# A Mamba-plus-cross-attention kernel on one Trainium2 core: TensorE's order inside a pair of units is alternated

## The reference, cut to what matters

```
for l in range(4):                      # Mamba layers
    x = rmsnorm(h); xi, z = split(x @ in_proj)
    xi = silu(causal_conv4(xi)); dt, B, C = split(xi @ x_proj); dt = softplus(dt @ dt_proj + b)
    for t in time:                      # 512 channels x 16 states
        s = exp(dt*A) * s + dt*B*xi     # the scan
        y = sum over the 16 states of s*C
    h = h + ((y + xi*D) * silu(z)) @ out_proj
h = rmsnorm(h)[:, 64:, :]
x = h + attention(layernorm(h), layernorm(ctx)) @ Wproj; x = x + mlp(layernorm(x))
```

## Time and profile before

| | |
|---|---|
| median of 3 runs | 9717.55 us (9715.33 to 9719.66) |
| the profiled execution, its own time | 9715.03 us |
| its span from first to last instruction | 9712.9 us |
| PE / DVE / ACT / POOL busy | 8902.0 / 7467.3 / 5988.0 / 6846.0 us |
| mean granted TensorE clock | 0.962 of full speed |

### The profile page before, as it was taken

The page is one execution under the profiler, slowest core; times in us unless marked ns, Lnnn a source line. Parts: engine busy times, 40 slices in busy tenths (PEclk is TensorE's granted clock), DMA queues, the critical chain, the costliest instruction groups (busy, mean ns, idle before and its releaser), DMA issues.

```text
span 9712.9 us, 193419 instructions
## 1 busy us (share of the span) xinstructions
PE 8902.0 (92%) x67488; PEld 6194.1 (64%) x67488; DVE 7467.3 (77%) x7810; ACT 5988.0 (62%) x9252; POOL 6846.0 (70%) x5860
## 2 busy tenths in 40 slices
PE   8999799999997899999997799999988799999988
PEld 5666466677664567677664566776654576766654
DVE  5778588888873588888873588888873688888872
ACT  6666576667753576676743566677642566776642
POOL 5888588888861488888861488888861588888850
PEclk9999899999999899999999899999999899999999
DMA  1111111111100111111100111111100111111100
GB/s 56 46 46 41 45 51 39 42 39 51 48 33 5 57 42 39 42 43 55 39 33 6 57 42 39 42 52 46 39 32 8 55 42 39 51 49 41 39 33 9
DMA packets 132829, 390.42 MB, mean 40 GB/s; under 512 B 49520, under 2 KB 77620, under 8 KB 94984
## 3 DMA queue, kind: packets, MB, share of 16 engines
q1 hardware_dynamic: 131848, 377.75, 10.9%
HBM read 364.46 MB, written 13.24 MB: 39 GB/s over the span
## 4 chain that ended last, share of the span: by engine, by line
POOL 51%; issue 36%; PE 3%; POOLq 1%; DVE 1%; ACT 0%; DVEq 0%; ACTq 0%
POOL arena L1139 43%; POOL arena L1146 4%; POOL arena L1158 2%; PE ps L540 1%; POOL arena L1176 1%; POOLq L1136 1%; PE ps L621 1%; DVE arena L1080 0%; DVE arena L1071 0%; ACT arena L824 0%; PE ps L517 0%; PE ps L587 0%; PE ps L437 0%; PE ps L616 0%; PE ps L454 0%
## 5 line engine op out<-in xcount | busy, mean ns | idle before, releaser
L1139 POOL TENSOR_TENSOR arena<-arena 128x512 f32<-128x512 f32 x4608 | 5765.3, 1276 | 1143.4 <-DVE arena L912 1103.9
L912 DVE TENSOR_TENSOR_SCAN arena<-arena,ps 128x512 f32<-128x512 f32 x4608 | 5610.4, 1259 | 785.6 <-PE ps L437 600.8
L673 ACT ACTIVATE arena<-arena,rate 128x512 f32<-128x512 f32 (+1 forms) x4608 | 3100.3, 713 | 801.8 <-DVE arena L912 789.8
L437 PE MATMUL ps<-arena 64*128 64x128 f32 x36864 | 2710.8, 287 | 313.8 <-DVE arena L912 306.4
L437 PEld LDWEIGHTS ps<-arena 64*128 64x128 f32 x36864 | 2266.9, 189 | 745.9 <-DVE arena L912 445.9
L454 PEld LDWEIGHTS ps<-csts,arena 128*128 128x128 f32 x18432 | 2128.5, 143 | 849.1 <-issue 629.5
L454 PE MATMUL ps<-csts,arena 128*128 128x128 f32 x18432 | 2466.4, 277 | 28.1 <-POOL arena L1139 27.4
L1158 POOL TENSOR_TENSOR arena<-arena 128x512 f32<-128x512 f32 x288 | 365.6, 1269 | 777.4 <-DVE arena L957 777.4
L1146 POOL TENSOR_TENSOR arena<-csts,arena 128x512 f32<-128x512 f32 x576 | 603.3, 1049 | 76.4 <-ACT arena L764 76.4
L517 PE MATMUL ps<-arena 128*128 128x512 f32 x1152 | 639.2, 649 | 7.6 <-DVE arena L962 4.4
L484 PE MATMUL ps<-arena 128*128 128x512 f32 x1152 | 636.0, 643 | 2.7 <-DVE arena L940 2.7
(11 more groups left out here) (102 smaller groups left out, 7510.2 us busy)
## 6 DMA issues: line engine op xcount, KB each, us to landing
arena<-c_rows SPq DMA_DIRECT2D x288, 1024.0 KB, 4.7
arena<-ip_x SPq DMA_DIRECT2D x20, 512.0 KB, 3.6
arena<-ip_z SPq DMA_DIRECT2D x20, 512.0 KB, 3.7
arena<-op_w SPq DMA_DIRECT2D x20, 512.0 KB, 3.8
hT<-xT SPq DMA_DIRECT2D x16, 512.0 KB, 5.1
arena<-w SPq DMA_DIRECT2D x8, 1024.0 KB
out<-arena SPq DMA_DIRECT2D x64, 128.0 KB, 1.7
arena<-xp_w SPq DMA_DIRECT2D x20, 160.0 KB, 2.4
```

Of the source, the lines that this page charges most:

```text
L437: i = nc.tensor.matmul(o, dtxT[rows, c, b, :], diagB[rows, pair, b, :].rearrange("p (i s) -> p i s", s=2), start=True, stop=True)
L673: nc.scalar.activation(o, i, ACT.Exp, scale=rate[:, ph.layer(n), g:g + 1]).then_inc(decay.sem, 1)
L912: nc.vector.tensor_tensor_scan(hs[:, place(n, v) + g % 2, :], dA[:, g % RING, :], both[:, g % 2::2], init[:, n % 2, g:g + 1] if ph.main() ...
L1139: nc.gpsimd.tensor_tensor(hs[:, a, :], hs[:, a, :], Crep[:, g % DS, :], ALU.mult).then_inc(prod.sem, 1)
```

## The change

TensorE's list alternates. In even units it stays: input of v+1, jobs of v, sum of v-2. In odd units it is turned round: sum of v-2, jobs of v, input of v+1. Nothing is added or removed, and no other engine's list is touched.

```
             def body(ph, n):
                 for v in range(UNITS):
-                    to, w = ahead(ph, n, v + 1)
-                    if to is not None:
-                        make_input(ph, to, w)
+                    ahead_of, behind = ahead(ph, n, v + 1), ahead(ph, n, v - 2)
+                    if ahead_of[0] is not None and v % 2 == 0:
+                        make_input(ph, *ahead_of)
+                    if behind[0] is not None and (scans(ph, n) or n == ph.steps) and v % 2:
+                        sum_pair(ph, *behind)
                     for m, name in events(ph.pe_at, ph, n, v):
                         job(ph, m, name)
-                    to, w = ahead(ph, n, v - 2)
-                    if to is not None and (scans(ph, n) or n == ph.steps):
-                        sum_pair(ph, to, w)
+                    if behind[0] is not None and (scans(ph, n) or n == ph.steps) and v % 2 == 0:
+                        sum_pair(ph, *behind)
+                    if ahead_of[0] is not None and v % 2:
+                        make_input(ph, *ahead_of)
```

## The result

The changed kernel takes 9861.24 us (median of 4 runs, 9860.55 to 9865.58), the kernel before 9718.6: ratio 1.0148, interval 1.013 to 1.0165. It is 1.5% slower. The forecast was 9783 us, 0.7% slower: right in direction and inside the range, but with less than half of the loss (65 of 143 us).

What follows compares the result with a forecast made beforehand. TensorE was taken to bound most of a main step, VectorE about a quarter. The profiled 9715 + 19 (main) + 31 (pre) + 15 (clock) = 9780, with 2.5 more for the median 9783 us; range 9685 to 9890.

Steps and rivals of the forecast that it cites:

- the order of events at units 14 to 17: Main step: input 16 comes 5.65 us after input 14, input 17 at 7.9 after 1.3 us of new idle time.
- trip: TensorE going into 64-row input matmuls and out again: about 0.4 us each, bounds 0.30 to 0.45; 16 instead of 32 a step.
- the undisturbed main step: Main step: 110.0 less 6.4 saved plus 6.7 new waits gives 110.3 us, +19 us over 64 steps.
- The waits of TensorE: Main step, ahead of inputs 3, 5, 7, 9, 17, 23, 25, 29, 31: 11.6 us instead of 4.9.
- The saving: TensorE's joints, every main and pre step: 16 x 0.4 = 6.4 us saved, bounds 4.8 to 7.2.
- the pre phase: 8 pre steps: each grows from 118.7 to 122.6 us by the sum, +31 us in all, bounds +16 and +60.
- The lump behind `out`: Pre step: input 6 moves from 695.27 to 702.9 behind the `out` jobs, making the scans of unit 7 2.1 us late.
- rival D: Main step: late GpSimd products stall sums ahead of an input, up to 0.5 us a step; 9815 us, chance 0.1.
- the clock: Main steps: new idle time brings some more half-speed stretches, 15 at 1 us each, +15 us.
- rival C: A half-speed stretch in each main step, where TensorE has no slack: 46 to 146 us more, 9860 us; chance 0.17.
- its sign, a mean clock under 0.95: Whole kernel: a mean TensorE clock below 0.95 would show the forecast wrong and point to rival C.
- the ends of the blocks: Last main steps and attention: no separate term; all 64 main steps at 0.3 us each, attention parts unchanged.

Runs made afterwards that it cites:

- e4: The changed kernel plus 14 unread identity transposes ahead of the input of unit 31, in all main steps but each block's last; 9789.56 us (1.0073).
- e10: The old order everywhere, plus 8, 10 and 8 unread identity transposes in units 4, 5 and 7 of each main step; 9706.94 us (0.9989).
- e11: The changed kernel with each block's last main step and the units that drain it put back in the old order; 9828.29 us (1.0114).
- e3: The kernel before with only units 7, 9, 11, 15 and 17 of each main step turned round, pre in the old order; 9614.9 us (0.9892).
- e6: The kernel before with the even units turned round instead of the odd ones, in both phases; 10115.5 us (1.0413).
- e7: The kernel before with units 4 to 10, 14, 16, 18 turned in main and 7, 10, 17, 18 in pre; 9730.54 us (1.0014).

## Why the prediction was right and wrong

**Right: the order of events at units 14 to 17.** The prediction put input 16 at 5.65 us behind input 14, and input 17 at 7.9 with 1.3 us idle. The timeline of PE in the changed kernel:

```profile
1406.50 1.91 PE L454 MATMUL ps<-csts,arena 128*128 128x128 f32 x16
1408.25 0.60 PE L510 MATMUL ps<-csts,arena 128*128 128x128 f32 x4
...
1409.64 2.06 PE L437 MATMUL ps<-arena 64*128 64x128 f32 x32
...
1415.29 1.16 PE L437 MATMUL ps<-arena 64*128 64x128 f32 x16
1417.58 1.16 PE L437 MATMUL ps<-arena 64*128 64x128 f32 x16 [1.13 <-DVE arena L915]
```

Input 16 comes at 5.65, input 17 at 7.94 with 1.13 us idle; two sums take 1.75 us, that is 2 x 0.88. In the old order input 17 comes 6.04 us behind input 15, with two jobs of the same kind and two sums between them (1601.72 to 1607.76 in the step of the earlier trace rows), so here one trip less is worth 0.39 us.

**Right by luck: the undisturbed main step.** The forecast was 110.0 - 6.4 + 6.7 = 110.3; measured are 110.6 (e4, at a clock of 1.00) against 110.0 (e10). But both terms were too large, and their errors nearly cancel. The waits of TensorE in that step of e4:

```profile
L437 PE MATMUL ps<-arena 64*128 64x128 f32 x514 | 35.9, 282 | 6.8 <-DVE arena L920 6.8
...
L490 PE MATMUL ps<-arena 128*80 128x512 f32 x8 | 3.9, 608 | 1.6 <-DVE arena L965 1.6
```

With 0.2 us ahead of `ms` and the 1.7 us that the filler covers they are 10.3 us, 5.5 more than the 4.8 of before and not 6.7 more. They stand where the forecast put them, ahead of the inputs 3, 5, 7, 17, 23 and 31, but for input 9: there the `xp` job waits in its place, for a bank, which the forecast did not have. The saving is what was mis-sized more: TensorE is busy 102.0 us, 100.3 without the filler, against 105.2, so 4.9 us are saved and not 6.4, that is 0.31 us a trip and not 0.4, at the lower end of the forecast's bounds. Why a trip is worth less on average than at units 14 to 17 no run shows.

Over the first 15 steps of the blocks the turned order costs 40 us (6628.6 in e4, 6588.4 in e10), where 64 steps were to give 19. Some 31 of it are the 0.6 us of 13 steps a block; about 5 lie in the first step of each block (109.7 against 108.5) and about 5 in the stretches that e4 still has.

**Right in its sum, with a wait that it did not have: the pre phase,** 29.8 us against 31, within the 8 us by which executions with this list differ, and 122.5 a step against 122.6. The lump behind `out` is there: in the timeline of DVE in a pre step of the changed kernel the scans of unit 6 start 6.53 us after the last of unit 5; the row gives no releaser, but their input starts at 722.70, behind the `out` jobs, and they follow it by 1.26.

```profile
714.00 3.43 DVE L915 TENSOR_TENSOR_SCAN arena<-arena,ps 128x512 f32<-128x512 f32 x3
723.96 1.22 DVE L915 TENSOR_TENSOR_SCAN arena<-arena,ps 128x512 f32<-128x512 f32 x1 [6.53 <-issue]
```

The input of unit 6 comes later than forecast, 10.9 us behind that of unit 5 and not 9.7, because the sum of unit 3, which now stands ahead of the jobs, waits for its product:

```profile
710.77 2.33 PE L437 MATMUL ps<-arena 64*128 64x128 f32 x32
...
715.24 0.66 PE L454 MATMUL ps<-csts,arena 128*128 128x128 f32 x4 [0.57 <-POOL arena L1142]
```

This is the mechanism of rival D, which the prediction looked for in the main steps. Up to the first main step the sums wait 45.6 us for GpSimd, against 11.5 before; in the first 15 steps of the first block it is 0.6 us.

**Wrong: the clock.** This is the term that was mis-sized: "I expect some more such stretches: 15 at 1 us each, **+15 us**". The prediction had found the idle time (2.2 us at unit 31; it is 1.95) and priced it in rival C, with 0.17. What came is rival C in kind, and by its sign, a mean clock under 0.95 (0.945): a stretch at unit 31 in three steps of four, on a stretch of the program where TensorE has no slack. That the time is also C's 9860 is luck, since C had 95 us of clock and nothing for the ends of the blocks. From the same sums, the stretches at unit 31 cost 59.5 us in the first 15 steps (6688.1 less 6628.6), those of the last steps 12 (4 x 3.0); the old order's own 17.7 go. Net 54 us, not 15. The step that failed was to count stretches by how rarely they came in the old order, once in three steps, and to price each at 1 us, the price where VectorE is the bound: the new ones follow the idle time that the new order creates at unit 31, and cost 1.6 us each. C's own argument named the 3.2 us of idle time at unit 5; that wait is there (3.03), but stretches around it cost 0.4 us at most (steps of 110.6 to 111.0 in e4).

**Wrong: the ends of the blocks.** All 64 main steps were priced alike and attention at nothing. The last step costs 4.2 us a block more, of which 3.0 is clock; the other 1.2 holds the order and what e4's own half-speed stretch there costs. The sum that waits for GpSimd ahead of an input (rival D) is real there as well. The part behind input 31 costs 4.5 us a block more; e11 gets some of it back (437.8 us in its first block, against 441.4). The order in it is not needed for such a loss: e3 has the old order there and still takes 12.5 us more than before in the four blocks. No run took the half-speed stretches of this part away, so the cause of these 18 us stays open.

The parts sum up: 30 pre, 40 main steps without the stretches at unit 31, 54 clock, 5 the rest of the last step, 18 behind it, 147 us of span.

Two slips in the prediction change nothing: `bT` does not use 128 rows either (80, in four records a step), and the lower end of rival C is 43 x 1.0 = 43 us, not 46.

## What to carry to other kernels

Grouping matmuls of one shape saves TensorE its joints (0.3 to 0.4 us a round trip here), but in a pipeline with a buffer for two units it turns even supply into lumps; turn only the units where the consumer has something left to do (in the same phase five of 32 gave 1.1%, sixteen lost 1.15%). When an order puts idle time (here 1.95 us) right in front of packed matmuls, look at the granted clock behind it, and price a stretch in every step; if it is there, a dozen transposes that nobody reads are cheaper than the stretch. A sum over durations is not enough: it must also hold every wait for a bank and for a product, since these are what e6, e7 and the pre steps ran into. The last turn of a loop has other cover than the rest and needs a sum of its own.

## What the runs showed that I had not expected

- Adding 14 transposes to each of 60 steps made the kernel 72 us faster.
- 1.95 us of waiting ahead of one input was followed by 3.41 us at 0.50, but in three steps of four only.
- The same order with the other parity (e6) is 2.6% slower than the changed kernel; it puts two users of one accumulator bank side by side, which waits 4.2 us in the main step shown.
- Pre steps charge 2.4 us for one turned unit (19 us in 8 steps) and 3.8 for sixteen (30 us).
- e7 comes out level (0.14% slower) because 52 us won in the main steps are lost again in 8 pre steps.
